# Delta mixer: GpSimd makes the two parts of the masked log decays, half a pair ahead, instead of VectorE

## What is computed

```python
def step(S, xs):
    qt, kt, vt, gt, bt = xs
    S = S * jnp.exp(gt)[..., None, None]
    kv = jnp.einsum('bhk,bhkv->bhv', kt, S)
    delta = (vt - kv) * bt[..., None]
    S = S + jnp.einsum('bhk,bhv->bhkv', kt, delta)
    o = jnp.einsum('bhk,bhkv->bhv', qt * scale, S)
    return (S, o)
...
g = -jnp.exp(A_log) * jax.nn.softplus(a + dt_bias)
```

## Time and profile before

| What | us |
|---|---|
| median of three runs | 4120.92 |
| lowest, highest | 4120.03, 4125.46 |
| the profiled execution | 4123.27 |
| its span in the trace | 4121.5 |
| PE busy in the span | 3729.6 (90%) |
| DVE busy | 2175.6 (53%) |
| ACT busy | 1713.0 (42%) |
| POOL busy | 500.4 (12%) |

### The profile page before, as it was taken

One profiled execution on the slowest core, in us unless ns is written; L12 is line 12 of the kernel. 1 busy time (PEld: TensorE's weight loads), 2 busy tenths in 40 slices (PEclk: granted clock), 3 DMA queues, 4 the chain that ended last, 5 costly groups with the idle time before them and its releaser, 6 DMA issues. The chain is left out here.

```text
span 4121.5 us, 57744 instructions
## 1 busy us (share of the span) xinstructions
PE 3729.6 (90%) x19926; PEld 2937.0 (71%) x19926; DVE 2175.6 (53%) x4780; ACT 1713.0 (42%) x4129; POOL 500.4 (12%) x344
## 2 busy tenths in 40 slices
PE   4847799999699999999999999999999998699998
PEld 2323478788478878778787787877878787588787
DVE  5547155555355464555645556455564555455554
ACT  3324222322155554554545546455554554323321
POOL 0102210200001010110101101111110110301200
PEclk8979899999799999999999999999999999899999
DMA  2010210210200000000000000000000000302210
GB/s 79 0 41 0 92 60 32 101 52 32 90 15 1 1 22 1 1 22 0 21 2 0 21 2 0 21 2 0 22 1 0 6 21 11 113 31 81 72 51 31
DMA packets 53735, 118.90 MB, mean 29 GB/s; under 512 B 2688, under 2 KB 3840, under 8 KB 52480
## 3 DMA queue, kind: packets, MB, share of 16 engines
q1 hardware_dynamic: 53504, 115.96, 7.9%
HBM read 90.78 MB, written 25.17 MB: 28 GB/s over the span
## 5 line engine op out<-in xcount | busy, mean ns | idle before, releaser
L1604 PE MATMUL banks<-b_x_cur,b_w_cur 128*128 128x256 f32 x2048 | 527.0, 386 | 7.9 <-ACT b_w_cur L1066 7.1
L1425 DVE COPY_PREDICATED b_Tt<-b_new_part,banks 128x256 f32<-128x256 uint8 x320 | 157.4, 492 | 674.8 <-PE banks L1676 674.8
L765 PE MATMUL banks<-f_x_hi,f_w_hi 128*128 128x512 f32 x1024 | 408.3, 399 | 38.8 <-ACT f_silu L634 21.7
L765 PE MATMUL banks<-f_x_lo,f_w_hi 128*128 128x512 f32 x1024 | 405.7, 396 | 0.0
L765 PE MATMUL banks<-f_x_hi,f_w_lo 128*128 128x512 f32 x1024 | 405.6, 396 | 0.0
L1604 PEld LDWEIGHTS banks<-b_x_cur,b_w_cur 128*128 128x128 f32 x2048 | 356.7, 191 | 48.7 <-issue 8.4
L1162 ACT COPY b_em<-banks 128x256 f32<-128x256 f32 x320 | 120.4, 376 | 548.2 <-PE banks L1662 548.2
L1662 PE MATMUL banks<-b_T,b_At 128*128 128x128 f32 x2560 | 345.9, 278 | 0.5 <-ACT b_T L1153 0.5
L1676 PEld LDWEIGHTS banks<-b_Tt,b_em 128*128 128x128 f32 x2560 | 332.0, 191 | 17.8 <-ACT b_em L1162 1.3
L1341 DVE SCALAR_TENSOR_TENSOR b_conv<-b_raw,b_taps,b_conv 128x256 f32<-128x256 f32 x768 | 334.8, 499 | 9.6 <-ACT b_conv L1103 9.6
L1676 PE MATMUL banks<-b_Tt,b_em 128*128 128x128 f32 x2560 | 338.1, 275 | 0.9 <-ACT b_em L1162 0.6
(11 more groups left out here) (256 smaller groups left out, 6620.4 us busy)
## 6 DMA issues: line engine op xcount, KB each, us to landing
f_x_tok<-rows SPq DMA_DIRECT2D x16, 1024.0 KB, 7.4
b_w_load<-in_b_qkvz SPq DMA_DIRECT2D x8, 1536.0 KB, 7.2
f_stage<-in_ffn_gate SPq DMA_DIRECT2D x8, 1024.0 KB, 6.6
f_stage<-in_ffn_up SPq DMA_DIRECT2D x8, 1024.0 KB, 7.5
f_stage<-in_ffn_down SPq DMA_DIRECT2D x8, 1024.0 KB, 4.9
f_x_res<-rows SPq DMA_DIRECT2D x8, 1024.0 KB, 5.5
f_part<-f_x_res SPq DMA_DIRECT2D x8, 1024.0 KB, 4.3
f_x_res<-f_part SPq DMA_DIRECT2D x8, 1024.0 KB, 5.5
```

Of the source, the lines that this page charges most:

```text
L765: mm = pe.matmul(bank, w[:, b, kind, cols], x[:, k, :], start=(k == 0 and i == 0), stop=(k == KD - 1 and i == 2))
L1425: dve.copy_predicated(half(f.Tt, i + 1, 1), new_part[:, i, :].rearrange("p (a n) -> p a n", n=LEVELS[i + 1]), half(f.right, i + 1, 1)).the ...
L1604: mm = pe.matmul(bank[i][:, 2 * part:2 * part + 2, :], w_cur[:, k, col:col + P], f.x_cur[:, k, :, :], start=(k == 0), stop=(k == KD - 1))
```

## The change

`log_decays` moves from DVE's program to POOL's, with the same arithmetic and shapes. POOL makes the parts of both flights of pair m + 1 in pair m, right behind `rsqrt_of_keys(B, m)` and ahead of both `chunk_of_x`; those of pair 0 it makes before the first pair, once DVE has written the tables (`CHAIN = 14` counts the steps of that).

```diff
+            def log_decays(f, m, h, c):
+                pool.wait_ge(f.s["dt"], m)
+                for out, part in ((f.g_hi, tab_hi), (f.g_lo, tab_lo)):
+                    pool.sem_inc(s["gate"], 1)
+                    pool.tensor_tensor(out[:, :, :].rearrange("p (b i) t -> p b i t", i=2),
+                                       upto[:, :].rearrange("p (b i t) -> p b i t", b=1, i=1)
+                                       .to_broadcast([P, BATCH, 2, P]),
+                                       part[:, :, bass.ds(c + f.i, 1), bass.ds(2 * h, 2)].rearrange("p b c i -> p b i c")
+                                       .to_broadcast([P, BATCH, 2, P]), ALU.mult).then_inc(f.s["gU"], 1)
...
                 masked_decay(B, m)
                 rsqrt_of_keys(B, m)
                 if not last:
+                    log_decays(A, m + 1, h + 1 if turn else h, 0 if turn else c + 2)
+                    log_decays(B, m + 1, h + 1 if turn else h, 0 if turn else c + 2)
+                if not last:
                     chunk_of_x(B, 1 if turn else c + 3, 2 * m + 2)
...
             chunk_of_x(A, 2, 1)
+            pool.wait_ge(s["chain"], CHAIN)
+            for f in flights:
+                log_decays(f, 0, 0, 0)
             pair(0, 0)
...
                 factors(A, m, h, c)
                 key_scales(A, m)
-                log_decays(B, m, h, c)
                 scales(A, m)
...
                 gated(B, m)
                 if not last:
-                    log_decays(A, m + 1, h + 1 if turn else h, 0 if turn else c + 2)
                     convolve(B, 2 * m + 3, 1)
                 mean_square(B, m)
...
-            log_decays(A, 0, 0, 0)
             pair(0, 0, first=True)
```

More of the change, by code:

```diff
@@ L858, in delta_mixer @@
     G_MIN = -104.0
+    CHAIN = 14
     with ExitStack() as ctx:
@@ L1350, in u4 @@
                 return ap.rearrange("p (b i) -> p b i", i=2)
[L1352 to L1360, removed]
             def factors(f, m, h, c):
```

## The result

| | us |
|---|---|
| before, median of 7 (lowest to highest) | 4120.92 (4120.03 to 4125.46) |
| after, median of 7 (lowest to highest) | 4136.85 (4132.54 to 4139.24) |
| ratio, with its 95% interval | 1.0035 (1.0024 to 1.0047) |
| span of the trace, before and after | 4121.5, 4135.1 |

The changed kernel is 15.9 us slower by the medians, 13.6 us by the spans of the two traces.

What follows compares the result with a forecast made beforehand. PE was taken as the bound, delayed by DVE's turns with POOL: 14 us lost less 5 gained gave +9, so 4123.27 + 9 = 4132 us. The range ran from 4114 to 4172.

Steps and rivals of the forecast that it cites:

- likeliest case: In `scales(B)`, `dcc` is shut out by the third product; `level(A, 0)` 0.45 us late in 31 pairs; 4132 us, chance 0.35.
- likeliest sign: Whole kernel: slower by over 0.2% was given 0.51, within 0.2% 0.37, faster 0.12.
- What bounds, and where it lands: Mixer: PE bounds; DVE's turns with POOL delay `level(A, 0)`, so PE's wait for it grows by about 14 us.
- Step 1: In `scales(B)`: the first product lets go at 2132.98, and `brk`, `nr` and `rqs` go in together.
- one turn more: Rival in `scales(B)`: `rqs` is shut out too, `level(A, 0)` 1.67 us late, +47 us, 4170 us; chance 0.15.
- The price: Each 128x512 product on POOL: 1.27 us taken, upper end 1.54, lower figure 1.15; 1.22 from start to start.
- The forecast case: In `scales(B)`: `rqs` gets in, `dcc` is held until 2135.42, `level(A, 0)` 0.45 us late; chance 0.35.
- loss at `level(A, 0)`: Flight B's `dcc` shut out ahead of it: 0.45 us late in each of 31 pairs, 14 us lost.
- openings of flight A: `brk` starts earlier; gain 0 in 8 pairs, 0.4 in 8, 0.1 in 15; about 4 us.
- first pair: PE's 3.9 us wait for `g_lo`: 1 us gained, between 0 and 3.9, since ACT is late next.
- end of the pair: Flight A's two products leave DVE, which then waits 1.2 us longer for ACT's squares: worth 0.

Runs made afterwards that it cites:

- experiment 1: Changed kernel, with all four GpSimd products moved behind the copy and a wait for flight B's first y product: 4111.14 us, ratio 0.9976 to before.
- experiment 2: Changed kernel, with flight A's two products left in place and flight B's two behind the copy and the late wait: 4118.01 us, ratio 0.9993 to before.
- experiment 3: Kernel before, VectorE still making its products, plus three unread GpSimd products a pair at the changed place: 4146.79 us, ratio 1.006 to before.
- experiment 4: Changed kernel, with only flight B's `dcc` moved on VectorE behind `matrices(B)`: 4111.05 us, ratio 0.9977 to before.
- experiment 5: Changed kernel with the log decays late, `masked_decay(B)` behind both powers, and flight B's copy behind the wait too: 4105.21 us, ratio 0.9958 to before.

## Why the prediction came out as it did

The time, 4136.85, is 4.9 above the forecast of 4132, inside its likeliest case's own range (4126 to 4138), and slower was the likeliest sign. But the path to it was partly another one, and two errors in its sum offset each other, which is luck. The closeness flatters it too. The forecast stood on the profiled execution, 2.35 above the median: the added time was put at 9, and the medians give 15.9. And the 0.79 us lost in a pair lies outside the 0.25 to 0.6 from which the case's own range was made.

*What bounds, and where it lands: as said.* The port is taken in turns, each for a whole instruction, let go 0.13 to 0.15 before the recorded end. The Trainium skill's rule (SBUF — State Buffer, § Who interferes with whom) that a DVE instruction with two SBUF inputs contends with a GpSimd instruction reading SBUF holds for `brk`, `ncc` and `dcc` at 0.96 to 0.99 us against 0.16. The loss appears as PE's wait for `level`, which grew by 24.9 where I had said about 14.

*Step 1 failed.* I let `brk`, `nr` and `rqs` in together behind the first product. `rqs` came 0.06 behind the second product's start (2138.39 against 2138.33) and was shut out: 1.01 us for two elements per partition. That is the mechanism of the rival "one turn more". Its reason, that an even one-input instruction within SBUF takes both read ports (the Trainium skill, VectorE: DVE Perf Modes, § Mode 2×_2P), agrees with the row of `rqs`; no run here tried it with an odd count, so the reason stays argued while the hold is shown.

*The price was off.* Products at 1.04 lie below even my lower end of 1.15. It made each turn 1.00 in place of 1.22, and this is what kept the extra turn from costing the rival's 1.67. From `brk`'s start I had for that rival three pitches of 1.22 and a first release at 1.04, with `level` 0.10 behind: 1.67 late. With the measured 1.00 and `brk` really starting 0.83 behind its recorded start it is 0.83 + 3 x 1.00 + 0.09 = 3.92, 0.79 late. The forecast case with that price and `rqs` let in would have had `dcc` done one turn sooner, at 2.92, before `level` was due at 3.13: no loss at all. The price alone would have made the kernel faster, the extra turn alone 47 us slower.

| term | said | measured |
|---|---|---|
| loss at `level(A, 0)` | 31 x 0.45 = 14 | 31 x 0.79 = 24.5 |
| openings of flight A | 4 | 5.3 |
| first pair | 1 | 0.4 |
| end of the pair | 0 | 0 |
| unassigned | | 2.4 gained |
| sum | +9 | +16.4, tables to last pair |

*The openings.* `Tt(A)` is ready earlier by 0.17, 0.04, 0.05 and 0.50 us in the first to the fourth pair of a head, and by 1.54 in the very first pair; these make 6.9, of which 1.6 ends in waits for ACT's squares. The kinds came out as predicted (0, about 0.1 for two of them, 0.4 for the last pair of a head): where `masked_decay(B)` holds L1418, an earlier start is worth nothing. In the last pair of a head L1418 comes later, so it is held for only 0.22 (0.91 in place of 0.69), and most of what `brk` gained gets through; before it wasn't held at all:

```profile
2282.54 0.91 DVE L1418 TENSOR_TENSOR b_Tt<-b_At,b_joins 128x512 f32<-128x512 f32 x1
```

*The end of the pair* was worth 0 as said: L1470 now waits 1.20 for ACT at 2120.38, where it was 0.23.

*The first pair.* PE's 3.9 for `g_lo` became 2.7 for ACT's `qkv`, 1.2 less; ACT was next, as said. Only 0.4 of it is left at the first `key_scales(A)`, which starts 28.26 us behind the writing of the tables before and 27.87 in the changed kernel, since DVE's wait there for ACT's squares grew from 3.29 to 4.09.

*The sum and the spans.* From the tables (L1322 before, at 1140.95) to the last pair the changed kernel is 16.4 longer, and the rows of the table add up to that. The spans differ by 13.6 only. When the tables were written, the changed kernel's execution was already 1.0 ahead. And behind the last level of the last pair it gained 2.3 on the same matmuls: TensorE's granted clock was 0.61 of full speed from 3488 to 3496 us in the trace of before, and 1.00 from 3504 to 3512, the same work, in the changed kernel's. Experiments 1 to 3 gained these 2.3 too, 4 and 5 did not, so they belong to the executions and not to the change. Experiment 1 checks the sum from the other side: without the loss it should be 5.3 + 0.4 + 2.4 = 8.1 faster than before from the tables to the last pair, and it is 8.5 (9.6 by the medians).

*What stays open.* The 2.4 us of gain lie in one step. In each pair that begins a head, except the very first, the fifth of the pair's masked copies (L1425 before, L1432 after) follows the fourth after 3.43 us in the kernel before and after 3.08 in the changed kernel: 7 x 0.35. TensorE is at work in between, and no wait shows it. Experiments 1, 2, 4 and 5 have 3.08; experiment 3, in which VectorE still makes its products, has 3.43. What makes the difference isn't known.

## What to carry to other kernels

In this kernel, work that moved from VectorE to GpSimd was not priced by its own length but by what VectorE did meanwhile. So count the long GpSimd instructions in a row and VectorE's instructions that need the shared port in that stretch, give each of the latter a whole one of the former, and see what is waited for behind the last of them. Here a chain of tiny scale computations was a bad neighbour. A stretch in which VectorE mostly waits for TensorE was a good one, and there the same products were worth 0.24%, and with the mask moved too 0.42%. Before giving up such a move, try its place, or moving the one small instruction at the end of the chain: each by itself recovered all of the loss.

## What the runs showed of the hardware

- Turns between the two engines were strict while GpSimd had instructions back to back: four of them let in VectorE's at 2138.23, 2139.24, 2140.23 and 2141.24. The next product starts within 0.1 us of each release, and a VectorE instruction that comes 0.06 behind that start is too late.
- A one-input instruction of 128x2, within SBUF, is held like the others: 1.01 us in place of 0.15 to 0.17. Those that read PSUM weren't: `level`'s masked copy and `Pt` took 0.71 each beside POOL's copy, and flight A's four of `At` 1.12 with `masked_decay(B)` running beside the second half of them.
- A 128x512 product on GpSimd takes 1.04 us if one input is a number repeated along the row, as long as its 128x1024 copy, and 1.27 with a mask or a full tile.
- VectorE with 128 instructions less showed 8 us more busy time; with the same instructions and the products in the quiet stretch (experiment 1) it shows 2108.8 us, 74.7 less.
